# Query bias added by a matmul in PSUM, and the high and low halves of the queries written straight from PSUM

## What is computed

```
q = (xn @ Wq + bq).reshape(b, h, t, dh)                 # 16 heads of 128: one head's queries mix tokens and slots
k = (xn @ Wk + bk).reshape(b, t, h, dh).transpose(0, 2, 3, 1)
v = (xn @ Wv + bv).reshape(b, t, h, dh).transpose(0, 2, 1, 3)
logits = einsum('bhtd,bhds->bhts', q, k) / sqrt(dh)
weights = softmax(logits + causal_mask)
attention = (weights @ v) merged over heads @ Wo + bo
```

## Time and profile before

| | us |
|---|---|
| median of 3 runs | 1937.94 (1934.93 to 1942.94) |
| profiled execution | 1938.18 |
| its span, first to last instruction | 1936.4 |
| TensorE matmul busy | 1670.1 (86%) |
| VectorE busy | 1539.5 (80%) |
| GpSimd busy | 1157.8 (60%) |
| ScalarE busy | 1087.6 (56%) |
| mean granted TensorE clock | 0.964 of full speed |

### The profile page before, as it was taken

The page is one execution under the profiler, slowest core; times in us unless marked ns, Lnnn a source line. Parts: engine busy times, 40 slices in busy tenths (PEclk is TensorE's granted clock), DMA queues, the critical chain, the costliest instruction groups (busy, mean ns, idle before and its releaser), DMA issues. The chain is left out here.

```text
span 1936.4 us, 49605 instructions
## 1 busy us (share of the span) xinstructions
PE 1670.1 (86%) x19088; PEld 1298.5 (67%) x19088; DVE 1539.5 (80%) x3187; ACT 1087.6 (56%) x2348; POOL 1157.8 (60%) x1005
## 2 busy tenths in 40 slices
PE   1499989999899999999877789989998999989996
PEld 1376766777677777777756667766676776667674
DVE  4888878888888888888854448988988898988885
ACT  0466556666566666666542236565665555566564
POOL 1146657777677777777660026666766666666653
PEclk9799999999999999999996779999999999999998
DMA  9455656565755556555557738777878787777864
GB/s 312 165 95 116 120 115 122 121 113 102 123 91 95 96 93 101 93 92 92 114 91 208 215 82 140 124 131 132 145 127 143 123 143 135 131 123 127 151 116 100
DMA packets 692691, 245.03 MB, mean 127 GB/s; under 512 B 643552, under 2 KB 680753, under 8 KB 691568
## 3 DMA queue, kind: packets, MB, share of 16 engines
q1 hardware_dynamic: 665584, 199.92, 56.0%
q0 software_dynamic: 18432, 33.64, 7.1%
q10 hardware_dynamic: 8448, 8.39, 1.3%
HBM read 57.11 MB, written 50.46 MB: 56 GB/s over the span
## 5 line engine op out<-in xcount | busy, mean ns | idle before, releaser
L479 POOL TENSOR_TENSOR prob<-prob 128x128 f16<-128x128 f32 (+7 forms) x512 | 659.9, 1292 | 619.5 <-ACT prob L855 613.2
L848 ACT ACTIVATE prob<-prob,nmax 128x128 f32<-128x128 f32 (+7 forms) x512 | 397.0, 775 | 648.1 <-DVE prob L1271 637.8
L690 PE MATMUL ps_s<-kT,qT 128*128 128x512 f16 (+3 forms) x2304 | 458.2, 326 | 9.8 <-DVE kT L1258 6.2
L705 PE MATMUL ps_o<-probT,vh 128*128 128x256 f16 (+1 forms) x3840 | 426.2, 264 | 3.9 <-DMA probT<-prob 3.9
L1271 DVE TENSOR_SCALAR_CACHE_REDUCE prob<-ps_s,neg_scale 128x128 f32<-128x128 f32 (+7 forms) x512 | 409.7, 808 | 3.3 <-PE ps_s L692 2.6
L705 PEld LDWEIGHTS ps_o<-probT,vh 128*128 128x128 f16 x3840 | 368.0, 99 | 48.1 <-issue 4.4
L855 ACT CAST prob<-prob 128x128 f16<-128x128 f32 (+7 forms) x512 | 341.4, 667 | 2.3
L690 PEld LDWEIGHTS ps_s<-kT,qT 128*128 128x128 f16 x2304 | 199.9, 98 | 149.4 <-issue 12.1
L719 PE MATMUL ps_y<-wo,oT 128*128 128x256 f16 x1536 | 211.3, 274 | 86.0 <-DVE oT L1286 68.7
L582 PE MATMUL ps_t<-xT,wq 128*128 128x64 f16 x6144 | 201.4, 195 | 60.5 <-DVE z L1173 23.6
L582 PEld LDWEIGHTS ps_t<-xT,wq 128*128 128x128 f16 x6144 | 192.4, 99 | 72.2 <-issue 29.8
(11 more groups left out here) (173 smaller groups left out, 1821.1 us busy)
## 6 DMA issues: line engine op xcount, KB each, us to landing
dispatched<-zeros SPq DMA_DIRECT2D x16, 512.0 KB, 14.6
probT<-prob SPq DMA_TRANSPOSE x512
ex<-dispatched SPq DMA_DIRECT2D x16, 512.0 KB, 4.3
expert_out<-eo ACTq DMA_DIRECT2D x16, 512.0 KB, 3.9
eup<-in_L_ffn_w_up_dram SPq DMA_DIRECT2D x64, 64.0 KB, 2.1
resid<-in_L_attn_x_dram SPq DMA_DIRECT2D x1, 3072.0 KB, 11.8
dispatched<-xn,slot_idx POOLq DMA_INDIRECT x192
xn_columns<-xnth SPq DMA_DIRECT2D x24, 128.0 KB
```

What stands on the lines that cost most here:

```text
L479: pool.tensor_tensor(low_cols(j), prob_cols(j).rearrange("p (r k) -> p r k", k=P), high_cols(j), ALU.subtract).then_inc(p_low, 1)
L690: pe.matmul(s_cols(j, lo, hi), qT[:, u, a, j * P:(j + 1) * P], kT[:, u, c, lo:hi], start=(n == 0), stop=(n == 2 and hi < w))
L705: mm = pe.matmul(ps_o[:, lo:2 * P], vh[:, u, a, r * D:(r + 1) * D], probT[:, PT_AT[c] + 2 * r + s, lo:], start=(r + n == 0), stop=(r == 2 ...
L848: nc.scalar.activation(prob_cols(j), prob_cols(j), ACT.Exp, bias=nmax[:, j:j + 1], scale=-1.0, accum_out=rsum[:, i % 2, j:j + 1]).then_inc ...
```

## The change

The bias of the queries is no longer added by VectorE. A matmul puts it into PSUM ahead of the projection: `bq_rows` holds the scaled bias as 16 rows of high halves and, from partition 32 on, 16 rows of low halves; `bq_pick` is a 0/1 matrix whose column m picks row m and row 32 + m; it is read with each column repeated 64 times. The matmul starts the accumulation of the whole bank, and the 48 matmuls of the projection add to it. The rows are built at the start: two small loads into a zero-filled tile, and three VectorE steps.

`full_q` and `qf` are gone. ScalarE's `high_q` now reads the PSUM bank and writes f16 in head order (elements 32 bytes apart). VectorE's `low_q` reads the PSUM bank and the high half, and writes the low half in head order. `project_k` and `project_v` wait for `q_low` where they waited for `q_full`. On ScalarE both `high_q` move up to right behind exponential 1 and `high_probs(1)`. On VectorE both `low_q` stand where the two `full_q` stood.

```diff
@@ sync
+            sp.wait_ge(bq_zero, 1)
+            for n in range(2):
+                sp.dma_start(bq_stage[32 * n:32 * n + H, :], bq.rearrange("(m d) -> m d", d=D)).then_inc(w_in, 16)
@@ gpsimd, first instruction
+            pool.memset(bq_stage[:], 0.0).then_inc(bq_zero, 1)
@@ tensor, project_q
+                if i == 0 and half == 0:
+                    pe.wait_ge(bq_step, 3)
+                pe.matmul(ps_t[:, half, :].rearrange("p (m t) -> p m t", t=TPH), bq_rows[:],
+                          bq_pick[:, half * (H // 2):(half + 1) * (H // 2)].unsqueeze(2).to_broadcast([P, H // 2, TPH]),
+                          start=True, stop=False)
...
-                                           xT[:, c, k, h * TPH:(h + 1) * TPH], start=(n + k == 0), stop=(n + k == 3))
+                                           xT[:, c, k, h * TPH:(h + 1) * TPH], start=False, stop=(n + k == 3 and m % (H // 2) == H // 2 - 1))
@@ tensor, project_k
-                    pe.wait_ge(q_full, 2 * i + half + 1)
+                    pe.wait_ge(q_low, 2 * i + half + 1)
@@ tensor, project_v
-                    pe.wait_ge(q_full, 2 * i + half + 3)
+                    pe.wait_ge(q_low, 2 * i + half + 3)
@@ tensor, scores
+                if j == 0:
+                    pe.wait_ge(q_low, 2 * i + 2)
                 if j % 4 == 0:
-                    pe.wait_ge(q_low, 2 * i + j // 4 + 1)
@@ scalar
             def high_q(i, half):
-                act.wait_ge(q_full, 2 * i + 2)
-                cols = slice(half * 512, (half + 1) * 512)
-                nc.scalar.copy(qT[:, i % 2, 0, cols], qf[:, cols]).then_inc(q_high, 1)
+                act.wait_ge(q_done, 2 * i + half + 1)
+                nc.scalar.copy(head_order(qT[:, i % 2, 0, :], half),
+                               ps_t[:, half, :].rearrange("p (m t) -> p m t", m=H // 2)).then_inc(q_high, 1)
@@ scalar, order within a head
+                    elif more:
+                        high_q(i + 1, 0)
                     high_probs(i, 1)
+                    if more and not swap:
+                        high_q(i + 1, 1)
                     softmax_exp(i, 2)
                     if old:
                         high_o(i - 1, 2)
-                    if more and not swap:
-                        high_q(i + 1, 0)
                     high_probs(i, 2)
                     softmax_exp(i, 3)
                     if not swap:
                         high_v(i, 0)
                         high_v(i, 1)
-                        if more:
-                            high_q(i + 1, 1)
+                    else:
+                        high_q(i + 1, 0)
                     high_probs(i, 3)
+                    if swap:
+                        high_q(i + 1, 1)
                     softmax_exp(i, 4)
@@ vector, at the start
-            wstep(V.tensor_scalar(bqT[:], bqT[:], scales[:, 0:1], None, ALU.mult))
+            V.tensor_tensor(bq_pick[:], ident[:, 0:H], ident[:, 32:32 + H], ALU.add).then_inc(bq_step, 1)
+            V.tensor_scalar(bq_rows[:], bq_stage[:], scales[:, 0:1], None, ALU.mult).then_inc(bq_step, 1)
+            dve.wait_ge(bq_step, 2)
+            V.scalar_tensor_tensor(bq_rows[32:32 + H, :], bq_stage[32:32 + H, :], scales[32:32 + H, 0:1], bq_rows[32:32 + H, :],
+                                   ALU.mult, ALU.subtract).then_inc(bq_step, 1)
@@ vector
-            def full_q(i, half):
...
+            def head_order(dst, half):
+                return dst.rearrange("p (t m) -> p m t", m=H)[:, half * (H // 2):(half + 1) * (H // 2), :]
 
             def low_q(i, half):
                 dve.wait_ge(q_high, 2 * i + half + 1)
-                cols = slice(half * 512, (half + 1) * 512)
-                V.tensor_tensor(qT[:, i % 2, 1, cols], qf[:, cols], qT[:, i % 2, 0, cols], ALU.subtract).then_inc(q_low, 1)
+                V.tensor_tensor(head_order(qT[:, i % 2, 1, :], half), ps_t[:, half, :].rearrange("p (m t) -> p m t", m=H // 2),
+                                head_order(qT[:, i % 2, 0, :], half), ALU.subtract).then_inc(q_low, 1)
@@ vector, order within a head
                     block_max(i, 0)
-                    low_q(i, 1)
...
                     elif more:
-                        full_q(i + 1, 0)
-                        full_q(i + 1, 1)
+                        low_q(i + 1, 0)
+                        low_q(i + 1, 1)
...
                     else:
-                        if more:
-                            low_q(i + 1, 0)
                         low_v(i, 0)
                         low_v(i, 1)
```

34 lines of the change are left out of this document (12 added, 22 removed).

## The result

The changed kernel takes 2210.7 us (median; 2209.8 to 2211.3) against 1936.4 of before: a ratio of 1.141, 95% interval 1.139 to 1.143. The forecast was 1980, the range 1932 to 2010. Slower was right; the size was not: +274 us where +42 were foreseen. The profiled execution has a span of 2209.5 us.

What follows compares the result with a forecast made beforehand. A relay between VectorE and ScalarE was taken to bound each head. Last stage 35.0, first stage 5.0, batch changes 3.6 and start -2 gave +41.6 us on 1938.18: 1979.8 us, range 1932 to 2010.

Steps and rivals of the forecast that it cites:

- The relay, and the shadows of the old low_q: Heads alternate between VectorE and ScalarE; the old `low_q` filled waits for ScalarE, so removing them gains 0.
- The upper bounds of a and d: Longest assumed times of the new `high_q` (a, 1.02 us) and new `low_q` (d, 1.36); 0.80 and 1.10 were taken.
- The walk from prices to the last stage: Last-stage `mix` starts 1.78 us later through the new evacuation, net 1.25 per head, x 28 = +35.0 us.
- The first stage, "no wait is exposed": Heads 0 to 33: `high_q` is done in time, only the `low_q` pair's pitch counts, 31 x 0.16 = +5.0 us.
- The give-back: GpSimd's pass comes 0.53 us earlier relative to the last-stage head, releasing the `mix` behind it that much earlier.
- TensorE, 0: The two added matmuls per head, 0.43 us, are covered by TensorE's waits of about 1.2 us: 0.
- The rival's 27: Rival that TensorE is late too: the added matmuls are uncovered, 27 us on top, 2007 us; chance 0.05.
- Start, -2: At the start the first `low_q` is no longer held by GpSimd, but `project_k` waits for both halves: about -2 us.
- The cheap hop: Rival: the new `high_q` and `low_q` both cost their lower bounds, 1933 us, no measurable change; chance 0.08.
- `yscale` ahead of GpSimd: Rival: `yscale` starts before GpSimd's pass, gaining 1.9 us in each of 28 last-stage heads, 1927 us; chance 0.09.
- Full relief: Rival: VectorE's saved 2.2 us per head count until TensorE binds, 62 x 0.77 = -48, 1890 us; chance 0.06.
- above the dearest prices (0.04): The part of the outcomes above the range's 2010 us, beyond the dearest assumed evacuation prices; chance 0.04.

Runs made afterwards that it cites:

- e3: The changed kernel with both evacuations walked row by row, so f16 is written in runs of 8 values; 1940.9 us, ratio 1.0014.
- e1: The kernel before plus trial 512-element operations behind its last head, on VectorE and ScalarE, in various access patterns; f16 written 32 bytes apart took 2342 ns on VectorE.
- e11: e3 with VectorE's small product `sh` moved ahead of `low_v`; 1932.7 us, ratio 0.9975.
- e9: The kernel before plus only the two added matmuls per head, here adding zeros ahead of `project_q`; 1942.7 us, ratio 1.0027.
- e13: The kernel before with `yscale` in a form that also writes an accumulator; 1894.0 us, ratio 0.978.

## Why the prediction was right in sign and wrong in size

*The relay, and the shadows of the old low_q.* Right. `low_k` starts 3.17 us into the head in before, after and e3; both waits for ScalarE grew as named.

*The upper bounds of a and d.* This is the step that failed, the prices of the new `high_q` (a) and the new `low_q` (d): "The upper bound is the 1.02 us which VectorE takes when each of 512 elements hops", and "two add at most 0.68". Measured were a = 2.31 us against 0.80 (bound 1.02) and d = 2.32 against 1.10 (bound 1.36). The hop of `full_q` was taken as a price per hop, whatever is written. It is a 4-byte write; the new ones are 2-byte writes, and e1 has 1.01 to 1.08 us for the one and 2.34 for the other on the same engine. The row was a neighbour in its pattern, not in its element size, and no other row of before wrote a lone 2-byte element. With no such row the honest range had no upper end; I took the nearest row for one. What the prediction cites has no such price either: the Trainium skill, Vector Engine (DVE) Microarchitecture Reference, section 5.2, measured 4-byte elements and gives 1.71 to 2.51 ns per element for a hopping output. `full_q`'s 0.34 us more over 512 elements agree with its 1.71 (against 1.05 in line), and the new write costs 4.6.

*The walk from prices to the last stage.* Right. With the measured a = 2.31 and d = 2.32 it gives: first `low_q` 1508.50 + 2.31 + 0.03 = 1510.84; second `high_q` ends 1513.43; `mix` at 1513.46 + 2.18 = 1515.64, 6.02 later than before; less 0.53 given back, 5.49, x 28 = +154. Measured: 5.22 a head and +147 for the stage. (0.2 of the difference is the gap between the two `high_q`: 0.11 us where the walk put 0.31.) With a = 0.58 it gave +0.43 and 0.37 came.

*The first stage, "no wait is exposed".* Wrong for a dear `high_q`: with it the pair waits 0.59 us in an odd interval (the heads with `slot_indices`) and 0.74 in an even one (those with the expert choice). Right for a cheap one (odd intervals of e3: no wait, -0.56, as the lower end had it). In even intervals two more terms were missed: `sh` losing 0.98 us to GpSimd's pass in e3, of which e11 gave 0.30 back, and TensorE's 0.37. Put together for after: pitch 2 x (2.18 - 0.88) = 2.60 in 31 heads, 81 us; waits of some 0.66 in 31, 20; `sh` 0.9 in 16, 14: 115 of the 119 measured. This is a sum of rows and not an experiment: that `sh` counts in full in the changed kernel is not shown, and neither is that e9's matmuls, which are left out of it, cost nothing there.

*The give-back.* The mechanism was right and counted on one side only. GpSimd's pass moves, and whether a step with two SBUF inputs meets it is a race in each place: `mix` won 0.5 us a head, `sh` lost 1.0.

*TensorE, 0.* Right in the last stage and in the odd intervals, from which its 1.18 us of wait were read the earlier trace rows; +5 us in the even ones (e9), of which the prediction showed no row. The rival's 27 did not come.

*Start, -2.* Right for the cheap form (e3 reached its first `block_max(7)` 4.1 us earlier); after came 3.7 later; that its dear instructions stand in line there is my reading, no run tests it.

*The rivals.* The cheap hop was false for the change as written and true for e3: e3 took 1941 where the rival gave 1933. There the first stage gave +1 instead of the -17 of that end. e3's profiled execution is 2.6 us longer than that of before: +1.4 and +10.5 in the two stages, -4.1 at the start, -0.8 at the end, and -4.4 in the expert stage, which kernels without the change show too. `yscale` ahead of GpSimd did not happen in after (it still took 2.09), but its price was right: 1.9 a head, "53 us" for the stage, e13 shows 44. Full relief: VectorE's relief did not count. But the reason given against more, that TensorE's mean wait of 1.2 us is all there is to take, was wrong: by its busy sum TensorE stands idle for 25.87 - 23.42 = 2.45 us of a last-stage head of before, and e13 took 1.87 of them. A case in which the prices lay beyond both bounds was given a chance of 0.04 ("above the dearest prices (0.04)") and no time, and it held nearly all of the miss.
